# A fused two-layer decoder on one Trainium2 core: moving the last attention's keys, values and map, and a few VectorE steps

## What is computed

```
x = x + L0_attn (layernorm(x))            # own attention, 16 heads, causal, keys and values gated by a line memory
x = x + L0_xattn(layernorm(x), ctx, ctx)  # heads over the context, 16 heads, rotary, causal
x = x + L0_ffn  (layernorm(x))            # rows quantised by their largest value, 3-tap convolution, silu
x = x + L1_attn (layernorm(x))            # second attention, 16 heads, not causal
x = x + L1_xattn(layernorm(x), ctx, ctx)  # last ("wide") attention: one head of 256 over the context
x = x + L1_ffn  (layernorm(x))            # experts, 2 of 16, and a shared one
```

```
k = einsum('bsd,ed->bse', key, Wk) + bk
v = einsum('bsd,ed->bse', value, Wv) + bv
scores = einsum('bqe,bke->bqk', q, k) / 16
probs = softmax(scores); return einsum('bqk,bke->bqe', probs, v)
```

## Time and profile before

| | |
|---|---|
| runs | 3309.21, 3306.66, 3306.17 us; median 3306.66 |
| the profiled execution's own time | 3310.13 us |
| its span | 3308.9 us, 47118 instructions |
| PE, PEld, DVE, ACT, POOL busy | 95%, 52%, 69%, 55%, 19% of the span |
| granted clock, mean | 0.996 |
| DMA | 148.57 MB, mean 45 GB/s |

### The profile page before, as it was taken

How to read it: one execution, slowest core, us unless ns; L and a number is a source line. 1 busy time by engine, 2 the same in 40 slices (tenths; PEclk the granted TensorE clock), 3 DMA queues, 4 the chain that set the end, 5 groups by cost and what they waited for, 6 DMA issues and landing times. The chain is left out here.

```text
span 3308.9 us, 47118 instructions
## 1 busy us (share of the span) xinstructions
PE 3153.9 (95%) x17628; PEld 1719.2 (52%) x17628; DVE 2277.3 (69%) x4243; ACT 1812.8 (55%) x2611; POOL 643.2 (19%) x1198
## 2 busy tenths in 40 slices
PE   6999999999999999999999999999999999999999
PEld 4544433378655453337864544334786444433487
DVE  6855688656685578856668457885667845798455
ACT  3565656643456565664355556566424656656632
POOL 0221010024122201012412120101341311100033
PEclk9999999999999999999999999999999999999999
DMA  3222022023031202111312120220232212021023
GB/s 137 50 34 42 1 37 33 14 65 112 31 59 27 40 1 39 31 37 59 111 35 45 19 40 1 46 33 29 74 96 42 40 21 37 15 34 33 10 86 97
DMA packets 124681, 148.57 MB, mean 45 GB/s; under 512 B 31577, under 2 KB 82113, under 8 KB 124173
## 3 DMA queue, kind: packets, MB, share of 16 engines
q1 hardware_dynamic: 124452, 145.56, 20.1%
HBM read 75.04 MB, written 4.46 MB: 24 GB/s over the span
## 5 line engine op out<-in xcount | busy, mean ns | idle before, releaser
L800 DVE TENSOR_REDUCE small<-psum 128x1 f32<-128x512 f32 (+6 forms) x1856 | 1127.1, 655 | 209.0 <-PE psum L650 190.8
L760 ACT ACTIVATE work<-psum 128x1024 f32<-128x1024 f32 (+5 forms) x1024 | 917.5, 935 | 423.0 <-PE psum L678 321.9
L650 PE MATMUL psum<-work 96*128 96x512 bf16 (+4 forms) x2688 | 645.0, 308 | 32.0 <-DVE small L800 16.7
L1968 PE MATMUL psum<-rounded_work 128*128 128x512 f32 x2592 | 600.2, 393 | 3.4 <-issue 3.4
L678 PE MATMUL psum<-work 99*128 99x512 bf16 (+4 forms) x2048 | 564.0, 358 | 15.1 <-ACT work L760 12.4
L1968 PEld LDWEIGHTS psum<-rounded_work 128*128 128x128 f32 x2592 | 489.9, 190 | 107.7 <-issue 5.2
L712 PE MATMUL psum<-work 128*32 128x512 f32 (+4 forms) x4480 | 508.4, 525 | 1.6 <-ACT work L760 1.5
L650 PEld LDWEIGHTS psum<-work 96*128 96x128 bf16 x2688 | 234.9, 97 | 522.2 <-DVE small L800 328.7
L678 PEld LDWEIGHTS psum<-work 99*128 99x128 bf16 (+1 forms) x2048 | 177.2, 97 | 198.3 <-ACT work L760 67.8
L2069 ACT CAST rounded_work<-work 128x512 fp32r<-128x512 f32 x144 | 89.4, 621 | 343.4 <-DVE work L2110 321.0
L850 POOL CAST small<-small 128x16 bf16<-128x16 f32 x96 | 18.8, 196 | 939.1 <-issue 569.5
(11 more groups left out here) (291 smaller groups left out, 3820.9 us busy)
## 6 DMA issues: line engine op xcount, KB each, us to landing
work<-work SPq DMA_DIRECT2D x640, 96.0 KB, 3.0
work<-combine SPq DMA_DIRECT2D x64, 512.0 KB, 4.1
work<-in_w_gate SPq DMA_DIRECT2D x64, 128.0 KB, 3.5
work<-in_w_up SPq DMA_DIRECT2D x64, 128.0 KB, 3.4
work<-in_w_down SPq DMA_DIRECT2D x64, 128.0 KB, 3.7
work<-in_x SPq DMA_DIRECT2D x8, 512.0 KB, 4.6
out<-x SPq DMA_DIRECT2D x8, 512.0 KB, 2.9
work<-work SPq DMA_DIRECT2D x128, 14.4 KB, 1.9
```

The lines of the kernel that those rows point to most:

```text
L650: ins = nc.tensor.matmul(dst[:, c * n:(c + 1) * n], A.q_pair[0:ROWS, slot, h, P * i:P * (i + 1)], A.k_of(pair, h)[0:ROWS, s0:s0 + n], star ...
L760: nc.scalar.activation(probs[0:size, n % PROBS, :, 0:P * many], banks(2 * (n % 2), 2)[0:size, :, 0:P * many], ACT.Exp, scale=DH ** -0.5).t ...
L800: nc.vector.tensor_reduce(tops[:, pair % 2, places[0]:places[-1] + 1:step], src, AX.X, ALU.max) \
L1968: ins = nc.tensor.matmul(dst, a_parts[i], b_parts[j], start=start and n == 0, stop=stop and n == 2, skip_group_check=True)
```

## The change

1. In the line memory, `lines_product(4)` and `(5)` come ahead of `scan_lines(0)` instead of behind it.
2. `wide` 0 to 3 leave the second attention's plan. Piece 0 (keys, bank 7) is issued on PE between the turning of the first four normed tiles and `cross_tensor(0)`, and taken out by ACT behind its copies of these tiles. Pieces 2, 3 (bank 7) and 1 (bank 0) are issued behind `cross_tensor(1)`; ACT takes them out behind all its cuts of the queries and ahead of the loading of the Exp table. The values' bias is added on POOL behind the context heads' work. Of 14 + 6 fillers 5 stay, and fillers of this stage write bank 3.
3. The transfer of `wide_q` is issued behind the own attention's last value and the context keys' transfers.
4. The results now lie in what were slots 4 and 5 of `probs`; the heads over the context and the second attention use 4 slots (`places`), the own attention 6.
5. The reduction of the rows' largest values is split: tiles 0 and 1 behind the third pair of statistics, 2 and 3 behind the last `norm_variance`, 4 to 7 where all eight were.

```diff
@@ norm_half @@
             norm_variance(tag, i0, HT)
+            if tag == "cross" and i0:
+                largest_of_rows(2, HT)
             norm_root(tag, i0, HT)
...
+        WIDE_MAP_AT = area.at - 2 * 2 * HALF
...
-        area.at = 0
+        area.at = WIDE_MAP_AT
         wide_kT, wide_map = (area.take(KD, S) for _ in range(2))
@@ class Heads @@
+                self.places = PROBS if tag == "own" else PROBS - 2
...
-                                    Heads("second", FULL, False, 10, q_pair, slot_keys, V, [("wide", n) for n in range(4)],
+                                    Heads("second", FULL, False, 10, q_pair, slot_keys, V, (),
@@ heads_tensor @@
-                busy_tensor(wait, 7)
+                busy_tensor(wait, 3 if a == "cross" else 7)
...
+                        elif a == "cross":
+                            pe.wait_ge(*at("wide_context", "cross", 1))
@@ heads_scalar @@
-                    if n >= PROBS:
-                        act.wait_ge(*at("valued", a, *A.order[n - PROBS][0:2]))
-                    nc.scalar.activation(probs[0:size, n % PROBS, :, 0:P * many], banks(2 * (n % 2), 2)[0:size, :, 0:P * many],
+                    if n >= A.places:
+                        act.wait_ge(*at("valued", a, *A.order[n - A.places][0:2]))
+                    nc.scalar.activation(probs[0:size, n % A.places, :, 0:P * many], banks(2 * (n % 2), 2)[0:size, :, 0:P * many],
@@ heads_sync @@
                         load_keys(A, pair)
+                    sp.wait_ge(*at("valued", "own", PAIRS_OF_HEADS - 1, NT - 1))
+                    nc.sync.dma_start(wide_q, io["wide_q"]).then_inc(*up("wide_q_landed", by=16))
...
-                    if a == "second" and pair == PAIRS_OF_HEADS - 2:
-                        for loaded in range(PAIRS_OF_HEADS - SLOTS, PAIRS_OF_HEADS):
-                            for h in range(2):
-                                sp.wait_ge(*at(LOADED[2 * (loaded % SLOTS) + h], a, loaded))
-                        nc.sync.dma_start(wide_q, io["wide_q"]).then_inc(*up("wide_q_landed", by=16))
@@ out_vector, out_scalar @@
+                if tag == "cross" and j == 2:
+                    largest_of_rows(0, 2)
...
+            if tag == "own":
+                wide_context_scalar(0, bank(7))
@@ gated_vector @@
-            for p in range(4):
+            for p in range(6):
                 lines_product(p)
             scan_lines(0)
-            lines_product(4)
-            lines_product(5)
             read_lines(0)
@@ cross_tensor @@
+                if n == 1:
+                    pe.wait_ge(*at("wide_context", "cross", 0))
@@ feed_vector @@
+        def largest_of_rows(i0, i1):
+
+            dve.wait_ge(*normed("cross", i1 - 1))
+            nc.vector.tensor_reduce(q_top[:, i0:i1], xn[:, i0:i1, :], AX.X, ALU.max, apply_absolute_value=True).then_inc(*up("vector_norm", "largest", i0))
...
-            own(nc.vector.tensor_reduce(q_top, xn[:, :, :], AX.X, ALU.max, apply_absolute_value=True))
+            largest_of_rows(HT, NT)
+            dve.wait_ge(*at("vector_norm", "largest", HT))
@@ wide_context_vector becomes wide_context_scalar: the same four on ACT, piece 1 without its bias @@
+                    ins = nc.scalar.activation(wide_kT[:, mm, :], src[:, S * mm:S * (mm + 1)], ACT.Identity, bias=resident["wide_kb"][:, mm:mm + 1])
...
+        def wide_values_gpsimd():
+            pool.wait_ge(*at("wide_context", "cross", 1))
+            for i, size in enumerate(CTX):
+                ins = nc.gpsimd.tensor_tensor(wide_v[0:size, i, :], wide_v[0:size, i, :], resident["wide_vb"][0:size, :], ALU.add)
+            ins.then_inc(*up("wide_biased"))
@@ tensor_program @@
             turn_tensor("own", 1)
+            pe.wait_ge(*at("gathered", "own", PAIRS_OF_HEADS - 1))
+            wide_context_tensor(0, bank(7))
             cross_tensor(0)
...
             cross_tensor(1)
-            pe.wait_ge(*at("cross_rotated", 0))
-            busy_tensor(14, cross_banks[0])
-            heads_tensor(cross_heads, cross_banks_free, 6)
+            pe.wait_ge(*at("cross_rotated", 1))
+            wide_context_tensor(2, bank(7)[:, 0:KD * S])
+            wide_context_tensor(3, bank(7)[:, KD * S:(KD + 1) * S])
+            pe.wait_ge(*at("cross_rotated", 2))
+            wide_context_tensor(1, bank(0))
+            heads_tensor(cross_heads, cross_banks_free, 5)
@@ scalar_program @@
             cross_scalar()
+            act.wait_ge(*at("wide_projected", 3))
+            wide_context_scalar(2, bank(7)[:, 0:KD * S])
+            wide_context_scalar(3, bank(7)[:, KD * S:(KD + 1) * S])
+            wide_context_scalar(1, bank(0))
             heads_scalar(cross_heads)
```

More of the change, by code:

```diff
@@ L700, in heads_tensor @@
                                 i0, _, many = A.steps[s][part]
-                                moving = probs[0:size, A.number[(pair, s, part)] % PROBS, h, 0:P * many]
+                                moving = probs[0:size, A.number[(pair, s, part)] % A.places, h, 0:P * many]
                                 dst = bank(7)[rows, P * (i0 // 2):P * (i0 // 2 + many)]
@@ L708, in heads_tensor @@
                                     continue
-                                moving = probs[0:size, A.number[(pair, s, 0)] % PROBS, h, 0:P * tiles].rearrange("p (i c) -> p i c", c=P)[:, j0::2, :]
+                                moving = probs[0:size, A.number[(pair, s, 0)] % A.places, h, 0:P * tiles].rearrange("p (i c) -> p i c", c=P)[:, j0::2, :]
                                 k0 = (i0 + j0) // 2
@@ L737, in heads_tensor @@
                 elif kind == "fill":
-                    busy_tensor(*key, 7)
+                    busy_tensor(*key, 3 if a == "cross" else 7)
                 elif kind == "late":
@@ L746, in heads_tensor @@
                     context_tensor(*key, take(kind, *key))
-                elif kind == "wide":
-                    wide_context_tensor(*key, take(kind, *key))
         def heads_scalar(A):
@@ L829, in heads_vector @@
                         keys_low(n)
-                elif kind == "wide":
-                    wide_context_vector(*key, bank(ring[(kind, *key)][0]))
         def heads_gpsimd(A, bias=None):
@@ L838, in heads_gpsimd @@
                     n, pair, s, _ = key
-                    block = probs[:, n % PROBS, :, 0:P]
+                    block = probs[:, n % A.places, :, 0:P]
                     pool.wait_ge(*at("prob", a, n))
@@ L1732, in wide_context_tensor @@
             else:
-                pe.wait_ge(*at("wide_context", "second", 0))
+                pe.wait_ge(*at("wide_context", "cross", 0))
                 if n == 2:
```

23 lines of the change are left out of this document (11 added, 12 removed).

## The result

| | before | after |
|---|---|---|
| runs, on the same chip | 3306.86 us (3304.35 to 3309.40, 6) | 3284.97 us (3283.91 to 3288.47, 6) |
| ratio, 95% interval | | 0.9937 [0.9927, 0.9946] |
| the profiled execution's own time, span | 3310.13, 3308.9 | 3283.91, 3282.6 |
| granted clock, mean | 0.996 | 0.998 |

21.9 us less, where 19.2 were forecast; 3287.5 us stood in the prediction, and 3280 to 3298 as its range.

The account below looks back on a forecast made before the run. PE, busy 95% of the span, was taken as the bound, with chains it waits for. Terms summed to -4.8 us a pass, -19.2 us over four passes, from 3306.66 to 3287.5 us; range 3280 to 3298.

Parts of the forecast that it names:

- products 4, 5 ahead: Line memory: the products fit into DVE's idle 1.94 us ahead of the scan; -0.7 us a pass.
- keys ahead of the queries: Ahead of the context heads: four wide matmuls in PE's 0.77 us wait, two ACT copies; +0.2 us a pass.
- map, row, values for fillers: Ahead of the context heads: ten matmuls and 5 fillers replace 20 fillers within the wait for a transfer; cost nothing.
- split reduction: Context heads to feed-forward: two parts lie in DVE's waits, the third takes 1.2 for 2.29 us; -0.8 us a pass.
- `wide_q` gone from pair 6: Second attention: without its 0.42 us issue, pair 6's rows' transfer goes out earlier and PE's wait goes; -0.45 us a pass.
- four pieces gone: Second attention's end: without the wide pieces' 5.23 us on PE, the last pair's first score runs earlier; -3.05 us a pass.
- the heads start when both are there, so the later one counts: Own heads' start: needs both DVE's chain to the keys (-0.7 us) and PE (-1.05 us); so -0.7 counts.
- the two delays overlap: Ahead of the context heads: PE's keys matmuls and ACT's copies each delay by +0.25 us, not added; +0.2 taken.
- context heads' start (1): Rival: packed transition makes PE reach the context heads' first piece 1.5 us late; 3293.5 us; chance 0.12.
- tail (2): Rival: second attention's end gives 2.4 instead of 3.05, products 0.3; 3291.7 us, or 3294 with dearer keys; chance 0.12.
- clock (3): Rival: new waits in tail and transition bring half clock; once a pass 3300.3 us (0.04), twice 3313 (0.03).
- four slots (4): Rival: four `probs` slots make Exps wait for values, lengthening ACT-bound stretches; no change in time; chance 0.01.

Follow-up runs that it names:

- run 1: The change with products 4 and 5 put back behind the first scan: 3286.43 us, ratio 0.9931 against the kernel before.
- run 6: The change with its keys piece made twice, on PE and ACT: 3295.68 us (one run).
- run 5: The change without the 5 fillers ahead of the context heads: 3284.69 us (one run).
- run 2: The change with the rows' largest values again in one DVE reduction behind all norms: 3292.97 us, ratio 0.9951 against the kernel before.
- run 4: The kernel before with the transfer of `wide_q` issued behind pair 6's rows instead of ahead: 3303.56 us, ratio 0.9985.
- run 12: The change itself, unaltered, measured once more against the kernel before: 3284.69 us, ratio 0.9922.
- run 7: The change with 3 slots for `probs` instead of 4 in the context heads and the second attention: 3423.04 us (one run).
- run 11: The change with two fillers behind the gates, ahead of the own heads: 3285.48 us, ratio 0.9927 against the kernel before.

## Why the prediction was right

Each term as forecast, and as the stages of the profile show it, per pass:

| term | forecast (bounds) | measured | shown by |
|---|---|---|---|
| products 4, 5 ahead | -0.7 (-0.3, -1.05) | -0.71 | run 1 |
| keys ahead of the queries | +0.2 (0, +0.8) | 0.0 | stage of 30.61 us; run 6 |
| map, row, values for fillers | 0 | 0 | run 5 |
| split reduction | -0.8 (-0.4, -1.1) | -0.93 | run 2 |
| `wide_q` gone from pair 6 | -0.45 (-0.3, -0.5) | -0.50 | run 4 |
| four pieces gone | -3.05 (-2.4, -4.3) | -3.20 | last `first` to output projection |
| sum | -4.8 | -5.3 | |

By the stages the gain is 2.2 us larger than the sum of the forecast, most of it from the keys (0.2 us a pass), the tail (0.15) and the reduction (0.13). Four passes give -21.4 us, the medians -21.9 and, in run 12's comparison, -24.1. The two profiled executions agree when the stretches at half clock are taken out: before 3310.13 - 9.9 = 3300.2 (1.7 + 3.2 + 1.8 + 3.2), after 3283.91 - 5.2 = 3278.7 (1.0 + 1.3 + 1.3 + 1.6).

- *The products.* The step "the heads start when both are there, so the later one counts" was right, to 0.01 us. What it left out is the clock behind the wait that takes DVE's place: stretches there in nine of ten passes, against one in three before. Estimated from these counts that is 1.3 x (29/32 - 4/12) = 0.75 us a pass at this place, as much as the 0.71 that the part gains, and run 1 can't be told from the change. But the whole time does not show this loss: the granted clock over the span is 0.9972 in the mean of the change's 11 executions and 0.9967 in that of 36 of the kernel before. So what the stretches take here the change does not lose in all; that this came out even is luck, since the sum has no term for the clock.
- *The keys.* The +0.2 was mis-sized, not mis-read: "the two delays overlap" is what happened. The recorded wait of 0.77 us did not show all of the room: PE's queries started 0.11 us later for 1.05 us of matmuls, and DVE's second rotation 0.03 us later. The bound of 0 was the right value. That it was on the edge shows only in run 6.
- *The fillers.* "4.8 us against 4.94 us until the transfer is there" held: the transfer sets the point, at 30.7 us. The ten matmuls took 3.51 us for 3.7 (which is 20 of 28 records' share of 5.23 us, and not, as written, what is left of it beside the 1.05 us of the keys, 4.18).
- *The reduction.* Part 2 was put at 0.3 us of overhang; it has 0.1, since it starts right behind the aggregation.
- *The tail.* The last pair's first score comes 5.42 us behind the last `first` for 8.46: 3.04 us, forecast 3.05. The transfer was used 2.27 us after its issue, forecast 2.25. The other 0.16 us arise between ACT's Exps of that score and the next four (5.13 us apart for 5.29), where the fourth piece stood, which was put at nothing.
  The Trainium skill, SBUF — State Buffer, section The DMA setup-cost knee, puts a small transfer at some 2 us; here it is 2.27, and the measurement decides.
- *The rivals.* The context heads' start (1) did not get dearer, the tail (2) gave all. The clock (3) fell at neither of the two places that it named, and not for its reason: tail and transition kept 1.00 with their waits of 0.3 to 0.8 us. It fell at a third place, where it cost 1.3 us and not 3.2. The four slots (4) don't bind; with three the forecast's sign would have turned.

## What to carry to other kernels

Work that does not depend on the rest can be put into another stage's waits for nothing, but only up to the room that is there, and the recorded wait does not tell it exactly (1.05 us of matmuls fitted where 0.77 us were recorded): double the moved piece once, and the edge shows. When a chain is shortened, look at the queue that feeds the next stage and at the order in which it issues: what is due first must not stand behind what is due last. Before a buffer is given away, try one slot fewer than planned, since the price can go from nothing to 33 us a pass in one step.

## What the runs showed of the hardware that was not expected

- The half-clock stretches stand at two places of the pass, and one more stands at the end of every span. With a wait of 0.4 to 0.7 us just ahead of the own heads one follows in 29 of 32 passes, while the waits of 0.3 to 0.8 us in the tail and the transition brought none but one in run 7's tail. PE was busy for all 3.50 us of the stretch at 912.50. At both places PE had just run through small matmuls: 16 records of 8 columns in 1.85 us (L1081) ahead of the own heads, 32 records of 16 columns in 3.64 us (the router's, at 3126.66 in the last pass) ahead of the stretch at the experts' start. Whether the wait alone brings the stretch, or the wait behind these, no run separates; the two fillers of run 11 change both. The Trainium skill, TensorE: Matmul & The Clock Gate, Part 1, says that the clock is lost when PE has been idle: the count goes that way at this place, with 0.5 us of idle time, and not at the others.
- The stretches were 3.4 or 6.8 us long in every kernel; with three slots, where ACT waits for a value of PE before each pair of Exps, there were 19 of them besides that at the end (mean clock 0.989).
- The issues of the queries' and keys' transfers take SP 0.6 us each even where nothing is waited for: twelve of them held back keys that were ready 1.2 us earlier.
